# A fused attention and mixture-of-experts block in fp32: the expert output product in scaled fp16 halves, and w1 tiles between the last gates

## Chip, cores and metric

One Trainium2 chip (trn2), one of its cores. The metric is device microseconds of one launch, from inputs in HBM to the output in HBM. Smaller is better.

## What is computed

The reference takes `x` of 16 images, 96 channels, 16x16 pixels, all fp32, and does two residual layers, each behind a group norm of 32 groups:

```
x = x + attention(gn(x))      # 1x1 conv to q,k,v; depthwise 3x3; l2-normed channel attention, 8 heads; 1x1 conv
x = x + experts(gn(x))

scores  = softmax(x_flat @ gate_w + gate_b)            # 4 experts, per pixel
top_w   = softmax(top 2 of scores)
present = which experts occur anywhere at rank 0, at rank 1
coef    = present(rank, expert) * top_w(rank, pixel), summed over the ranks
hdn     = relu(w1[e] @ x + b1[e])                      # 4 x 96 hidden rows
out     = sum over e of coef[e] * (w2[e] @ hdn[e] + b2[e])
```

## The kernel before

The work goes by pairs of images: 8 pairs of 512 pixels (`T`). The engines are programmed by hand: each block (`tensor`, `vector`, `scalar`, `gpsimd`, `sync`) is one in-order list, and semaphores carry the dependences. Nothing is scheduled by a planner; the order of the code is the order of the queue.

First comes the attention layer, one pair per turn of a loop. PE makes q and k with the depthwise filter folded into nine shifted products (`conv_taps`, L721 to L737, fp16 halves of operands), projects v (`project_v`, L778), and makes the small products of the heads. DVE does the other eight taps of v (`taps`, L1150), the statistics (L1106) and the head arithmetic; `project_v(i + 1)` waits for all taps of pair i (`tap_done`). ACT makes the centre tap, copies q and k out of PSUM and rounds the normalised x to fp16; POOL subtracts for the low halves (L619, L624) and takes roots; SP packs the halves by DMA. The weights of the second layer are prepared in pairs 0 and 1: PE turns w1 and w2 (`prepare_late`, L699 to L702), ACT copies them (`copy_late`), DVE makes the low half of w1 (`low_w1`, L1086).

Then come the gates and the hidden layer. `gate(p)` (L835) is 4 fp32 products of four columns each. `first(h)`, h = 3 x pair + m for three blocks m of 128 hidden rows, is a w1 tile: three fp16 products of 512 columns (L850 to L852) into one of four banks, emptied by a relu of ACT (L511) or, for h in `RELU_DVE`, of DVE (L1215). DVE ranks the experts per pixel in two chunks of four pairs each (`gate_logits`, `gate_compare`, `gate_rank`, `gate_present`, `gate_scores`, `gate_weights`, `gate_parts`), where `present` of both chunks gives the counts on PE (L937, L940). `gate_parts` splits the two weights of a pixel into bf16 parts and copies them to `u_tok`, which PE turns into `u_sb` (`turn_u`, L928, and `take_u` on ACT, L524).

Last comes the second phase, per pair i (`second`, L975 and L979; DVE `mix` L1411 and `add` L1417): PE spreads the coefficients of the next pair over 128 rows (`coef`, L960), DVE multiplies them into the hidden values (`h_mixed`, two buffers), PE makes three fp32 products with w2 and one bf16 product for the bias, and DVE adds the result to x. POOL prepares the bias rows before it (L678 to L686). The last pair goes in two halves of 256 pixels (`last_second`, L989 and L990, L1436).

## Time and profile before

| | |
|---|---|
| median of 3 runs | 181.02 us (179.81 to 182.39) |
| the profiled execution | 178.98 us |
| its span in the trace | 177.2 us |
| PE, DVE, ACT, POOL busy | 161.3, 139.4, 89.1, 50.4 us |
| granted TensorE clock, mean | 0.981 |

All rows further down come from that one profiled execution. Times are us from the start of its span. A matmul's duration includes the way through the array, so neighbours overlap; the distance between their starts says what one costs PE in a stream. The granted clock is 1.00 at 2.4 GHz and 0.50 at 1.2 GHz. "[1.03 <-DVE present]" behind a row is idle time of the engine just before it, and what ended it.

### The profile page before, as it was taken

The page shows a single profiled execution, that of the slowest core. Times are in us where ns is not written, and L with a number is a line of the kernel's source. Part 1 is how long each engine was busy: PE and PEld are TensorE (multiplying, and loading weights), DVE is VectorE, ACT ScalarE, POOL GpSimd, SP SyncE. Part 2 cuts the span into 40 slices and gives each one's busy share as a digit, 9 for nine tenths or more (in the row PEclk, how much of TensorE's full clock was granted, in tenths as well). Part 3 has the DMA queues.
Part 4 walks back from the last instruction along what each step waited for, and adds up shares of the span by engine and source line. Part 5 has one row for each costly group of instructions (what it writes and reads, how often), then busy time and mean ns, then how long its engine had stood idle before and what let it go on. Part 6 is the DMA issues. An engine that isn't in the chain of part 4 may idle for free.

```text
span 177.2 us, 3598 instructions
## 1 busy us (share of the span) xinstructions
PE 161.3 (91%) x1313; PEld 119.1 (67%) x1313; DVE 139.4 (79%) x383; ACT 89.1 (50%) x206; POOL 50.4 (28%) x74
## 2 busy tenths in 40 slices
PE   0567988999989999899999999999979999999994
PEld 0556978999989899899999987667225423222232
DVE  2589999979999999988998894776894697566641
ACT  2083298749284592984954485636965323100000
POOL 5120222605143144432472363243520510000000
PEclk9999999999999999999999999999579999999999
DMA  6994123411405014040050000000000002011113
GB/s 149 240 226 97 29 72 80 113 42 36 117 0 137 17 35 121 0 135 19 10 145 0 6 0 0 2 4 0 0 0 0 4 0 62 27 44 44 48 45 89
DMA packets 8810, 9.71 MB, mean 55 GB/s; under 512 B 3640, under 2 KB 7512, under 8 KB 8792
## 3 DMA queue, kind: packets, MB, share of 16 engines
q1 hardware_dynamic: 8648, 9.25, 21.0%
q8 instruction: 10, 0.16, 0.4%
q10 hardware_dynamic: 144, 0.23, 0.3%
q14 instruction: 8, 0.07, 0.1%
HBM read 2.93 MB, written 1.57 MB: 25 GB/s over the span
## 4 chain that ended last, share of the span: by engine, by line
PE 51%; DVE 31%; issue 5%; ACT 4%; DMA 4%; POOL 2%; SPq 2%; DVEq 0%; POOLq 0%
DVE v_acc L1150 10%; PE mix_ps L975 7%; PE v_ps L975 5%; PE qk_ps L732 5%; PE qk_ps L734 5%; DVE stats L1106 3%; PE out_ps L821 3%; PE qk_ps L960 3%; DMA x_sb<-in_x 2%; PE sc_ps L786 2%; DVE wc L1037 2%; PE sc_ps L796 2%; POOL rstd L639 2%; PE qk_ps L737 2%; DMA x_c<-x_lo 1%
## 5 line engine op out<-in xcount | busy, mean ns | idle before, releaser
L1150 DVE SCALAR_TENSOR_TENSOR v_acc<-v_ps,v_taps,v_acc 96x576 f32<-96x576 f32 x64 | 51.8, 809 | 2.0 <-ACT v_acc L439 0.8
L732 PE MATMUL qk_ps<-w_a,x_a 128*128 128x192 f16 x243 | 46.6, 245 | 0.5 <-DMA x_c<-x_lo 0.5
L734 PE MATMUL qk_ps<-w_b,x_b 128*128 128x192 f16 x243 | 46.5, 245 | 0.0
L732 PEld LDWEIGHTS qk_ps<-w_a,x_a 128*128 128x128 f16 x243 | 24.6, 101 | 1.1 <-issue 0.8
L734 PEld LDWEIGHTS qk_ps<-w_b,x_b 128*128 128x128 f16 x243 | 23.6, 97 | 0.3
L737 PE MATMUL qk_ps<-w_c,x_c 96*128 96x192 f16 x81 | 20.1, 248 | 0.0
L630 POOL TENSOR_TENSOR sq_sum<-qk_sq 128x384 f32<-128x384 f32 x8 | 8.0, 999 | 30.5 <-ACT qk_sq L447 26.8
L1411 DVE TENSOR_TENSOR h_mixed<-hidden,qk_ps 128x512 f32<-128x512 f32 x16 | 10.7, 682 | 6.5 <-PE qk_ps L960 6.5
L485 ACT ACTIVATE sc_exp<-sc_qk,neg_max 96x12 f32<-96x12 f32 x16 | 4.7, 296 | 18.6 <-DVE neg_max L1189 18.5
L1106 DVE BATCH_NORM_STATS2 stats<-x_sb 96x6 f32<-96x256 f32 x32 | 11.6, 412 | 2.9 <-DMA x_sb<-in_x 2.7
L639 POOL TENSOR_TENSOR rstd<-var_eps,minus_half 96x4 f32<-96x4 f32 (+2 forms) x9 | 9.0, 996 | 17.1 <-DVE var_eps L1132 17.1
L975 PE MATMUL mix_ps<-h_mixed,w2T 128*96 128x512 f32 x24 | 13.2, 631 | 0.0
L634 POOL TENSOR_TENSOR rnorm<-norm,minus_half 96x4 f32<-96x4 f32 x8 | 8.1, 1013 | 15.3 <-DVE norm L1159 15.3
L624 POOL TENSOR_TENSOR xn_lo<-xn,xn_hi 96x512 f16<-96x512 f32 x8 | 9.3, 1166 | 10.3 <-ACT xn_hi L506 10.2
L619 POOL TENSOR_TENSOR x_lo<-xs,x_a 96x512 f16<-96x512 f32 x8 | 9.3, 1160 | 8.3 <-ACT x_a L467 8.3
L721 PE MATMUL qk_ps<-w_a,x_a 96*128 96x192 f16 x45 | 11.1, 246 | 0.5 <-ACT w_a L432 0.5
L459 ACT ACTIVATE xs<-x_sb,shift,rstd 96x256 f32<-96x256 f32 x16 | 8.7, 596 | 4.9 <-DVE shift L1138 4.9
L723 PE MATMUL qk_ps<-w_a,x_lo 96*128 96x192 f16 x45 | 11.1, 246 | 0.0
L722 PE MATMUL qk_ps<-w_b,x_a 96*128 96x192 f16 x45 | 11.1, 246 | 0.0
L975 PE MATMUL v_ps<-h_mixed,w2T 128*96 128x512 f32 x18 | 9.9, 631 | 0.0
L500 ACT ACTIVATE xn<-x_sb,shift,rstd 96x256 f32<-96x256 f32 x16 | 8.5, 590 | 1.1 <-DVE shift L1138 1.1
L446 ACT COPY qk_sb<-qk_ps 128x384 f32<-128x384 f32 x16 | 7.5, 469 | 3.1 <-PE sc_ps L796 2.9
(226 smaller groups left out, 365.6 us busy)
## 6 DMA issues: line engine op xcount, KB each, us to landing
x_b<-x_a SPq DMA_DIRECT2D x7, 324.0 KB, 3.1
x_sb<-in_x SPq DMA_DIRECT2D x8, 192.0 KB, 4.9
out<-xs SPq DMA_DIRECT2D x7, 192.0 KB, 2.1
x_a<-x_lo SPq DMA_DIRECT2D x7, 108.0 KB, 2.6
x_b<-x_lo SPq DMA_DIRECT2D x7, 108.0 KB, 2.3
x_c<-x_lo SPq DMA_DIRECT2D x21, 36.0 KB, 1.9
wdw_all<-in_L_conv_w_dw SPq DMA_DIRECT2D x1, 648.0 KB, 5.8
w_sb<-in_L_conv_w SPq DMA_DIRECT2D x2, 144.0 KB
```

What stands on the lines that cost most here:

```text
L619: eng.tensor_tensor(inner(x_lo[p], 1), xs[p][:, :].rearrange("c (b h w) -> c b h w", b=2, w=W), inner(x_a[p], 1), ALU.subtract).then_inc(l ...
L639: eng.tensor_tensor(rstd[:, lo:hi], var_eps[:, lo:hi], minus_half[:, 0:hi - lo], ALU.pow)\
L721: eng.matmul(to, hi, w_a[0:C, t, :], start=(t == 0), stop=False, skip_group_check=True)
L722: eng.matmul(to, hi, w_b[0:C, t, :], start=False, stop=False, skip_group_check=True)
L723: mm = eng.matmul(to, lo, w_a[0:C, t, :], start=False, stop=(t == TAPS - 1), skip_group_check=True)
L732: eng.matmul(to, window(x_a[p][:, dx, b], half, dy), w_a[:, t, :], start=(t == 0), stop=False, skip_group_check=True)
L734: mm = eng.matmul(to, window(x_b[p][:, dx, b], half, dy), w_b[:, t, :], start=False, stop=False, skip_group_check=True)
L737: mm = eng.matmul(to, window(x_c[p][:, b], half, dy), w_c[:, dy, :], start=False, stop=(t == TAPS - 1), skip_group_check=True)
L975: eng.matmul(to, w2T[:, m, :], h_mixed[i % 2][:, m, :], start=(m == 0), stop=False, skip_group_check=True)
L1106: s = eng.bn_stats(stats[:, at + b, :], x_sb[:, i, b * HW:(b + 1) * HW])
L1150: eng.scalar_tensor_tensor(out=v_acc[i % 3][:, :, :], in0=v_window(dy, dx), scalar=v_taps[:, t:t + 1], in1=v_acc[i % 3][:, :, :], op0=ALU. ...
L1411: eng.tensor_tensor(h_mixed[i % 2][:, m, :], hidden[:, i, m, :], coef_ps[m], ALU.mult)\
```

## The change

Part one, the gates: `first(10)` and `first(11)` go between gates 5, 6 and 7, and two more w1 tiles go ahead of the wait for `present`. ACT takes two relus earlier. On DVE `gate_parts` is divided into `gate_split` and the copies; for chunk 0 the copies go behind `gate_present(1)`.

Part two, the second phase: w2, with the factor of w1 already in it, is scaled per output channel to a largest value of 1024 and turned back; its first block stays fp32 (`w2_full`), the other two become fp16 halves (`w2_hi`, `w2_lo`). This takes a turn on PE, six operations on DVE, another turn, three copies on ACT and a subtraction on DVE, all in pairs 1 and 2. Per pair, ACT then rounds blocks 1 and 2 of `h_mixed` to fp16 (`high_mixed`), POOL subtracts for the low half, and PE makes one fp32 product, and hi x hi, lo x hi and hi x lo for each of two blocks. The product of the two low halves is not made. The addition multiplies by `w2_back`. The new buffers lie in `wc`, `wdw_all`, `x_a` and `x_b`, free by then. Before, no engine but PE and DVE worked on a pair in the second phase.

The diff, cut (declarations, semaphores and the second of two like places are left out):

```diff
+W2_SCALE = 1024.0
...
-                eng.copy(wprojT[:, :], out_ps[0:C, 0:C])
+                eng.copy(wprojT[:, :], out_ps[0:C, 0:C]).then_inc(late_set, 1)
                 for m in range(MT):
                     a = eng.activation(w2T[:, m, :], out_ps[:, C * (m + 1):C * (m + 2)], ACT.Copy,
                                        scale=w1_back[:, m:m + 1])
-                a.then_inc(late_set, 1)
+                a.then_inc(w2T_set, 1)
+
+            def high_w2():
+                eng.wait_ge(b2_turned, 1)
+                eng.copy(b2_rows[:, :], out_ps[0:EXPERTS, MT * C:(MT + 1) * C]).then_inc(b2_rows_set, 1)
+                eng.copy(w2_full[:, :], out_ps[:, 0:C])
+                eng.copy(w2_hi[:, 1:MT, :], out_ps[:, C:MT * C].rearrange("p (m o) -> p m o", m=MT - 1)).then_inc(w2_hi_set, 1)
+
+            def high_mixed(i):
+                wait(eng, y_done, i - 1)
+                wait(eng, h_lo_set, 2 * (i - 1))
+                for m in range(1, MT):
+                    eng.wait_ge(mixed_done, MT * i + m + 1)
+                    eng.copy(h_hi[i % 2][:, m, :], h_mixed[i % 2][:, m, :]).then_inc(h_hi_set, 1)
...
             for i in range(PAIRS):
                 centre_tap(i)
+                if i == 2:
+                    high_w2()
...
             normalise2(5)
             normalise2(6)
+            relu(7)
             normalise2(7)
-            relu(7)
+            relu(8)
...
                 relu(h)
             eng.wait_ge(bias_done, 1)
             eng.copy(bias32[:, :], small_ps[0:U, BIAS:BIAS + C]).then_inc(bias_copied, 1)
+            take_u(1)
+            high_mixed(0)
             top_exps(1)
-            take_u(1)
+            high_mixed(1)
             take_u(2)
             take_u(3)
+            for i in range(2, PAIRS):
+                high_mixed(i)
 
...
+            for i in range(PAIRS):
+                wait(eng, y_done, i - 1)
+                for m in range(1, MT):
+                    eng.wait_ge(h_hi_set, 2 * i + m)
+                    eng.tensor_tensor(h_lo[i % 2][:, m, :], h_mixed[i % 2][:, m, :], h_hi[i % 2][:, m, :],
+                                      ALU.subtract).then_inc(h_lo_set, 1)
...
+            def turn_w2():
+
+                eng.wait_ge(w2T_set, 1)
+                eng.wait_ge(w1_lo_set, 1)
+                for m in range(MT):
+                    eng.transpose(mix_ps[0:C, m * 128:(m + 1) * 128], w2T[:, m, :], const("ident", 128))
+                eng.transpose(mix_ps[0:C, ED:ED + EXPERTS], b2_sb[:, :], const("ident", EXPERTS)[:, 0:EXPERTS])\
+                   .then_inc(w2_turned, 1)
+
+            def turn_w2_again():
+                eng.wait_ge(b2_cols_set, 1)
+                for m in range(MT):
+                    eng.transpose(out_ps[:, m * C:(m + 1) * C], w2_scaled[:, m, :], const("ident", C)[:, 0:C])
+                eng.transpose(out_ps[0:EXPERTS, MT * C:(MT + 1) * C], b2_cols[:, :], const("ident", C)[:, 0:C])\
+                   .then_inc(b2_turned, 1)
...
-                    eng.wait_ge(w1_lo_set, 1)
+                    eng.wait_ge(b2_cols_set, 1)
...
+                if i == 1:
+                    turn_w2()
...
+                if i == 1:
+                    turn_w2_again()
...
             first(9)
             gate(5, 0, 8)
+            first(10)
             gate(6, 0, 8)
+            first(11)
             gate(7, 0, 8)
-            for h in (10, 11, 12, 13, 14, 15):
+            for h in range(12, 18):
                 first(h)
 
...
 
-            first(16)
-            first(17)
+            first(18)
+            first(19)
             eng.wait_ge(present_ready, 1)
             eng.wait_ge(norm_done, 9)
...
-            first(18)
-            first(19)
+            first(20)
+            first(21)
...
             turn_u(0)
             turn_u(1)
-            for h in range(20, HT):
+            for h in range(22, HT):
...
-                for m in range(MT):
+
+                coef(i + 1, 0)
+                eng.wait_ge(mixed_done, MT * i + 1)
+                eng.matmul(to, w2_full[:, :], h_mixed[i % 2][:, 0, :], start=True, stop=False, skip_group_check=True)
+                for m in range(1, MT):
                     coef(i + 1, m)
-                    eng.wait_ge(mixed_done, MT * i + m + 1)
-                    eng.matmul(to, w2T[:, m, :], h_mixed[i % 2][:, m, :], start=(m == 0), stop=False,
+                    eng.wait_ge(h_hi_set, 2 * i + m)
+                    eng.matmul(to, w2_hi[:, m, :], h_hi[i % 2][:, m, :], start=False, stop=False,
+                               skip_group_check=True)
+                    eng.matmul(to, w2_lo[:, m, :], h_hi[i % 2][:, m, :], start=False, stop=False,
                                skip_group_check=True)
                 if i == 0:
                     eng.wait_ge(bias_ready, 1)
-                eng.matmul(to, bias_u[:, :], u_sb[:, i * T:(i + 1) * T], start=False, stop=True,
-                           skip_group_check=True).then_inc(y_done, 1)
+                eng.matmul(to, bias_u[:, :], u_sb[:, i * T:(i + 1) * T], start=False, stop=False,
+                           skip_group_check=True)
+                for m in range(1, MT):
+                    eng.wait_ge(h_lo_set, 2 * i + m)
+                    mm = eng.matmul(to, w2_hi[:, m, :], h_lo[i % 2][:, m, :], start=False, stop=(m == MT - 1),
+                                    skip_group_check=True)
+                mm.then_inc(y_done, 1)
...
+            def scale_w2():
+
+                eng.wait_ge(w2_turned, 1)
+                eng.tensor_reduce(w2_top[:, :], mix_ps[0:C, 0:ED], AX.X, ALU.max, apply_absolute_value=True)\
+                   .then_inc(w2_step, 1)
+                eng.wait_ge(w2_step, 1)
+                eng.tensor_scalar(w2_floor[:, :], w2_top[:, :], TINY, 1.0 / W2_SCALE, ALU.max, ALU.mult)\
+                   .then_inc(w2_step, 1)
+                eng.wait_ge(w2_step, 2)
+                eng.reciprocal(w2_scale[:, :], w2_floor[:, :]).then_inc(w2_step, 1)
+                eng.wait_ge(w2_step, 3)
+                eng.reciprocal(w2_back[:, :], w2_scale[:, :])
+                eng.tensor_scalar(w2_scaled[:, :, :], mix_ps[0:C, 0:ED].rearrange("p (m d) -> p m d", m=MT),
+                                  w2_scale[:, 0:1], None, ALU.mult)
+                eng.tensor_scalar(b2_cols[:, :], mix_ps[0:C, ED:ED + EXPERTS], w2_scale[:, 0:1], None, ALU.mult)\
+                   .then_inc(b2_cols_set, 1)
+
+            def low_w2():
+                eng.wait_ge(w2_hi_set, 1)
+                eng.tensor_tensor(w2_lo[:, 1:MT, :], out_ps[:, C:MT * C].rearrange("p (m o) -> p m o", m=MT - 1),
+                                  w2_hi[:, 1:MT, :], ALU.subtract).then_inc(w2_lo_set, 1)
...
-            def gate_parts(c):
+            def gate_split(c):
                 t = chunk(c)
-                n = t.stop - t.start
                 step(eng.tensor_copy(tw_hi[:, :, t], top_w[:, :, t]))
                 step(eng.tensor_tensor(tw_rest[:, :, t], top_w[:, :, t], tw_hi[:, :, t], ALU.subtract))
                 step(eng.tensor_copy(tw_mid[:, :, t], tw_rest[:, :, t]))
                 step(eng.tensor_tensor(tw_lo[:, :, t], tw_rest[:, :, t], tw_mid[:, :, t], ALU.subtract))
+
+            def gate_parts(c):
...
+                if i == 2:
+                    low_w2()
...
-                taps(i, 6, 8)
+                taps(i, 6, 7)
+                if i == 1:
+                    scale_w2()
+                taps(i, 7, 8)
...
+            gate_split(0)
             gate_compare(1)
             gate_beaten(eng, 1)
             gate_rank(1)
             gate_present(1)
+            gate_parts(0)
             relu(16)
 
...
             def mix(i):
                 wait(eng, y_done, i - 1)
+                wait(eng, h_lo_set, 2 * (i - 1))
                 for m in range(MT):
...
             def add(i):
                 eng.wait_ge(y_done, i + 1)
                 wait(eng, stored[i % 2], 16 * (i // 2))
-                eng.tensor_tensor(out_sb[i % 2][:, :], x_sb[:, i, :], y_ps[i % 2][0:C, :], ALU.add)\
-                   .then_inc(y_taken, 1)
+                eng.scalar_tensor_tensor(out=out_sb[i % 2][:, :], in0=y_ps[i % 2][0:C, :], scalar=w2_back[:, 0:1],
+                                         in1=x_sb[:, i, :], op0=ALU.mult, op1=ALU.add).then_inc(y_taken, 1)
...
             gate_parts(1)
```

The order on each engine, as the two programs have it, at three places.

DVE at the end of pair 1, before, from the head factors on (`v_acc` is a tap, `x2` two in a row):

```order
L1172 TENSOR_TENSOR k_diag<-cst,rnorm 96x24
L1175 TENSOR_SCALAR q_fac<-rnorm,temp_sb 96x2
L1150 SCALAR_TENSOR_TENSOR v_acc<-v_ps,v_taps,v_acc 96x576 x2
L1138 SCALAR_TENSOR_TENSOR shift<-small_ps,rstd 96x4
L1180 TENSOR_TENSOR sc_k<-picked,sc_ps 96x24
L1186 TENSOR_TENSOR sc_qk<-sc_k,q_fac 96x24
```

and after (here `w_top` to `w_back` are the `w2_` tiles, whose numbers the listing leaves out):

```order
L1292 TENSOR_SCALAR q_fac<-rnorm,temp_sb 96x2
L1267 SCALAR_TENSOR_TENSOR v_acc<-v_ps,v_taps,v_acc 96x576
L1187 TENSOR_REDUCE w_top<-mix_ps 96x1
L1190 TENSOR_SCALAR w_floor<-w_top 96x1
L1193 RECIPROCAL w_scale<-w_floor 96x1
L1195 RECIPROCAL w_back<-w_scale 96x1
L1196 TENSOR_SCALAR w_scaled<-mix_ps,w_scale 96x384
L1198 TENSOR_SCALAR b_cols<-mix_ps,w_scale 96x4
L1267 SCALAR_TENSOR_TENSOR v_acc<-v_ps,v_taps,v_acc 96x576
L1255 SCALAR_TENSOR_TENSOR shift<-small_ps,rstd 96x4
L1297 TENSOR_TENSOR sc_k<-picked,sc_ps 96x24
```

Six operations now stand between tap 7 and tap 8.

PE around the last gates, before (`gate_w_sb` is a gate, three rows with `w_hi`, `w_lo`, `w_hi` a w1 tile):

```order
L852 MATMUL qk_ps<-xn_lo,w_hi 128x512
L835 MATMUL mix_ps<-gate_w_sb,xn_1 128x4 x4
L835 MATMUL mix_ps<-gate_w_sb,xn_2 128x4 x4
L835 MATMUL mix_ps<-gate_w_sb,xn_3 128x4 x4
L850 MATMUL v_ps<-xn_hi,w_hi 128x512
L851 MATMUL v_ps<-xn_hi,w_lo 128x512
L852 MATMUL v_ps<-xn_lo,w_hi 128x512
```

and after:

```order
L924 MATMUL qk_ps<-xn_lo,w_hi 128x512
L907 MATMUL mix_ps<-gate_w_sb,xn_1 128x4 x4
L922 MATMUL v_ps<-xn_hi,w_hi 128x512
L923 MATMUL v_ps<-xn_hi,w_lo 128x512
L924 MATMUL v_ps<-xn_lo,w_hi 128x512
L907 MATMUL mix_ps<-gate_w_sb,xn_2 128x4 x4
L922 MATMUL v_ps<-xn_hi,w_hi 128x512
L923 MATMUL v_ps<-xn_hi,w_lo 128x512
L924 MATMUL v_ps<-xn_lo,w_hi 128x512
L907 MATMUL mix_ps<-gate_w_sb,xn_3 128x4 x4
L922 MATMUL qk_ps<-xn_hi,w_hi 128x512
```

The three gates are apart by a w1 tile each.

ACT from the last relus on, before:

```order
L511 ACTIVATE hidden<-v_ps,b_scaled 128x512 x2
L597 COPY bias<-small_ps 12x96
L520 ACTIVATE top_exp<-top_diff 128x16
L524 COPY u_sb<-out_ps 12x1024
L524 COPY u_sb<-sc_ps 12x1024
L524 COPY u_sb<-out_ps 12x1024
```

and after (`x_a<-wc` and `x_a<-wdw_all` are `high_mixed` of an even and an odd pair):

```order
L552 ACTIVATE hidden<-v_ps,b_scaled 128x512 x2
L640 COPY bias<-small_ps 12x96
L565 COPY u_sb<-out_ps 12x1024
L469 CAST x_a<-wc 128x512 x2
L561 ACTIVATE top_exp<-top_diff 128x16
L469 CAST x_a<-wdw_all 128x512 x2
L565 COPY u_sb<-sc_ps 12x1024
L565 COPY u_sb<-out_ps 12x1024
L469 CAST x_a<-wc 128x512 x2
```

The roundings of pair 0 stand behind one `u_sb` copy, those of pair 1 ahead of the last two, and those of pair 2 behind all of them.

## Rows read from the trace of the kernel before

**Rows 1.** Chain of waits of core 0, 38 to 60 us, its shares by line.
```profile
by line: DVE v_acc L1150 46.2%; issue 14.4%; DVE stats L1106 11.6%; DVE picked L1167 4.3%; DVE attn L1197 4.0%; DVE x_sb L1155 2.8%; DVE masked L1163 2.5%; DVE mv L1120 2.1%; DVE sc_qk L1186 1.7%; DVE neg_max L1189 1.6%; ACT sc_exp L485 1.5
```

**Rows 2.** Timeline of DVE, pair 1: start, duration (us), line, operation, shapes.
```profile
21.98 0.17 DVE L1072 TENSOR_SCALAR w_row_max<-w_top 128x3 f32<-128x3 f32 x1
...
30.36 0.54 DVE L1086 TENSOR_TENSOR w_lo<-mix_ps,w_hi 96x384 f16<-96x384 f32 x1
...
33.62 0.34 DVE L1163 TENSOR_TENSOR masked<-sc_ps,cst 96x192 f32<-96x192 f32 x1
...
35.42 1.65 DVE L1150 SCALAR_TENSOR_TENSOR v_acc<-v_ps,v_taps,v_acc 96x576 f32<-96x576 f32 x2
```

**Rows 3.** Timeline of PE: weight transposes, and the projection of pair 2.
```profile
25.02 0.25 PE L699 MATMUL out_ps<-cst,wproj_sb 96*96 96x96 f32 x1
...
25.61 0.25 PE L702 MATMUL out_ps<-cst,w_sb 96*128 96x96 f32 x1
...
37.22 0.28 PE L778 MATMUL v_ps<-x_a,wv_hi 96*96 96x256 f16 x1
```

**Rows 4.** Timeline of ACT: one rounding of 96x512.
```profile
124.78 0.60 ACT L506 CAST xn_hi<-xn 96x512 f16<-96x512 f32 x1
```

**Rows 5.** Gate stretch: PE, then PEclk by window (start:end, busy times), DVE, POOL.
```profile
120.06 3.02 PE L835 MATMUL mix_ps<-gate_w_sb,xn 96*128 96x4 f32 x24 [0.31 <-ACT xn L500]
...
128.32 0.63 PE L852 MATMUL v_ps<-xn_lo,w_hi 96*128 96x512 f16 x1
...
131.14 0.38 PE L851 MATMUL qk_ps<-xn_hi,w_lo 96*128 96x512 f16 x1
131.35 0.38 PE L852 MATMUL qk_ps<-xn_lo,w_hi 96*128 96x512 f16 x1
132.76 0.20 PE L937 MATMUL small_ps<-present,ones 128*12 128x8 f32 x2 [1.03 <-DVE present L1256]
...
124.00:126.00 2.00, 2.00 (x6) 0.33 (x4) 1.49 (x7) 1.91 (x5) 0.54 (x1) 0.50 0.00 0
...
113.44 0.23 DVE L1230 TENSOR_TENSOR g_in<-logits,g_max 128x64 f32<-128x64 f32 x1
...
125.60 1.10 DVE L1230 TENSOR_TENSOR g_in<-logits,g_max 128x64 f32<-128x64 f32 x1
...
125.46 1.15 POOL L624 TENSOR_TENSOR xn_lo<-xn,xn_hi 96x512 f16<-96x512 f32 x1 [4.26 <-ACT xn_hi L506]
```

**Rows 6.** Timeline of DVE and POOL: taps beside a subtraction.
```profile
39.72 4.19 DVE L1150 SCALAR_TENSOR_TENSOR v_acc<-v_ps,v_taps,v_acc 96x576 f32<-96x576 f32 x5
...
41.45 1.16 POOL L619 TENSOR_TENSOR x_lo<-xs,x_a 96x512 f16<-96x512 f32 x1 [0.64 <-ACT x_a L467]
```

**Rows 7.** Second phase: busy times of one window, then PE, ACT, POOL, DVE.
```profile
160.00:170.00 10.00, 10.00 (x24) 2.50 (x24) 6.16 (x10) 0.00 (x0) 0.00 (x0) 1.00 0.21 59
...
144.00 0.41 PE L979 MATMUL mix_ps<-u_sb,bias_u 12*96 12x512 bf16 x1
...
149.61 0.39 PE L960 MATMUL qk_ps<-u_sb,spread 12*128 12x512 bf16 x1
149.92 1.10 PE L975 MATMUL mix_ps<-h_mixed,w2T 128*96 128x512 f32 x2
150.95 0.39 PE L960 MATMUL qk_ps<-u_sb,spread 12*128 12x512 bf16 x1
...
153.65 0.41 PE L979 MATMUL mix_ps<-u_sb,bias_u 12*96 12x512 bf16 x1
153.90 0.37 PE L960 MATMUL qk_ps<-u_sb,spread 12*128 12x512 bf16 x1
...
149.26 1.00 ACT L524 COPY u_sb<-sc_ps 12x1024 bf16<-12x1024 bf16 x1 [5.84 <-PE sc_ps L928]
...
142.13 0.40 POOL L686 TENSOR_TENSOR bias_u<-bias_d,bias_c 12x96 bf16<-12x96 f32 x1
...
174.61 0.42 DVE L1436 TENSOR_TENSOR xs<-x_sb,mix_ps 96x256 f32<-96x256 f32 x1 [1.28 <-PE mix_ps L990]
```

More of the change, by code:

```diff
@@ L112, in build @@
         w2T = sb("w2T", [128, MT, C])
+        w2_top = sb("w2_top", [C, 1])
+        w2_floor = sb("w2_floor", [C, 1])
+        w2_scale = sb("w2_scale", [C, 1])
+        w2_back = sb("w2_back", [C, 1])
+        w2_scaled = sb("w2_scaled", [C, MT, 128])
+        w2_full = sb("w2_full", [128, C])
+        w2_hi = sb("w2_hi", [128, MT, C], F16)
+        w2_lo = sb("w2_lo", [128, MT, C], F16)
+        b2_cols = sb("b2_cols", [C, EXPERTS])
+        b2_rows = sb("b2_rows", [EXPERTS, C])
         x_sb = sb("x_sb", [C, PAIRS, T])
@@ L579, in _ @@
             normalise2(6)
+            relu(7)
             normalise2(7)
-            relu(7)
+            relu(8)
             top_exps(0)
-            relu(8)
             high_xn2(5)
@@ L1285, in gate_parts @@
                 step(eng.tensor_tensor(tw_lo[:, :, t], tw_rest[:, :, t], tw_mid[:, :, t], ALU.subtract))
+            def gate_parts(c):
+                t = chunk(c)
+                n = t.stop - t.start
                 for part, at, k in ((tw_hi, 0, 3), (tw_mid, 3, 2), (tw_lo, 5, 1)):
```

57 lines of the change are left out of this document (40 added, 17 removed).

## The prediction

> **What bounds the kernel now.** I read the chain of waits first, then the timeline of each engine in three places, then the busy time by stage. The kernel has three stretches with different limits.
>
> From 25 to 60 us the chain runs on VectorE (DVE): between 38 and 60 us its largest parts are the depthwise taps `v_acc`, the statistics, and the small head operations, all DVE [rows 1]. TensorE (PE) is nearly as full, but it waits at the end of each pair: the projection of pair 2 starts at 37.22, 0.15 us after the last two taps of pair 1 end (35.42 + 1.65 = 37.07) [rows 2, 3]. So what is put into DVE's queue here goes to the end of the kernel, and what is put into PE's queue here is free only as far as DVE is later.
>
> Up to 133 us the limit is then the gate chain, again on DVE. PE runs the three last gates from 120.06 as 24 products of four columns, and a few us later its granted clock is 0.50, the 1.2 GHz level: a 512-column product takes 0.63 us at 128.32 and 0.38 at 131.14 [rows 5]. This looks like the price of the stretch, but PE then sits idle for 1.03 us until `present` is there, and starts the counts at 132.76 [rows 5]. PE at half clock was still early. What DVE lost is in the same group: `g_in` took 0.23 us at 113.44 and 1.10 at 125.60, and the long one ended (126.70) just after a POOL subtraction that had started at 125.46 ended (126.61). The Trainium skill has a rule for this ("SBUF — State Buffer", Who interferes with whom): a VectorE operation with two SBUF inputs and a GpSimd operation that reads SBUF shut each other out for a whole instruction. The trace agrees.
>
> From 140 us on PE is the limit: busy 10.00 us of 10 between 160 and 170, DVE 6.16 [rows 7]. A pair takes 4.29 us there, from the coefficient product at 149.61 to the same one of the next pair at 153.90. It is three times an fp32 product of 1.03 us (149.92 to 150.95) and a coefficient product of 0.32, plus 0.25 for the bias product [rows 7].
>
> **The preparation of the halves (pairs 1 and 2), on DVE.** `scale_w2` stands between tap 7 and tap 8 of pair 1, six operations. Reduction and scaling over 96x384 read from PSUM: the row of that width is `w_lo`, 0.54 us. The reduction must end before the next starts: 0.57; the scaling overlaps its neighbour by 0.08: 0.46. Three small ones in a chain at 0.17 and a gap of 0.03, the last without the gap: 0.5; `b2_cols` 0.1. Together 1.6 us. `low_w2` in pair 2 covers 128x192 like `masked` (0.34, of which 0.28 is not overlapped): 0.3. Sum 1.9 us, all in front of the tap on which the next projection waits [rows 2]. PE gets eight transposes; seven like them stand between 25.02 and 25.61 at 0.1 us each, so 0.8 us [rows 3]. They lie beside the 1.6 of DVE and cost nothing more while DVE is later; uncovered they cost 0.8. ScalarE (ACT) gets three copies (`high_w2`), about 0.5 us together since a 96x512 copy takes 0.60 [rows 4]; they stand behind DVE's chain in front of `take_qk` and the packing of pair 3, and might add 0.2. Bounds: 1.6 (if pair 2 absorbs its part) to 2.7 (if PE's transposes come on top). I take **+1.9**, the value of the DVE rows.
>
> **The gate stretch.** Gates 5, 6 and 7 get a w1 tile between them. Gate 7 ends 1.3 us later, near 124.3 (24 products from 120.06 took 3.0), still ahead of DVE, which works on those logits from 125.60. The clock may stay up, worth some 3 us of PE, but PE is not what is waited for. DVE's chain to `present` loses only the three copies to `u_tok`, an estimated 0.3 us of work of their own, three at 0.1 beside each other; the three POOL subtractions still meet two-input operations in it (`tw_rest`, `beats`, `tied` instead of the copies), so I let the three waits stand. Two more w1 tiles run before the wait, four instead of six remain behind it (saves 1.3). But the first of these four waits for `relu(16)`, now queued behind the `u_tok` copies (0.3) and itself some 0.7 long over its 512 columns, of which PE waits about 0.7, and ACT must still do five relus after `take_u(0)`, which comes 0.3 to 0.6 later against `present`. I take **-0.4** for the start of the second phase. Bounds: -3.2 (all POOL waits missed and the clock up) and +0.6 (ACT's queue decides and no wait is missed).
>
> **Second phase, first three pairs.** PE's products of a pair are now one fp32 (1.03), the coefficient product before it (0.32), and nine products at 16 bits: 131.14 to 131.35 is 0.21 each, so 1.94. Sum 3.29 instead of 4.29 [rows 5, 7]. But pair 0 ends with two low products that wait for POOL. POOL's bias work ends at 142.13 + 0.40 = 142.53 and only then come the two subtractions. One of 96x512 took 1.16 us [rows 6], width and types are the same here: 2.3 us, then the product, 0.4. That is 145.3, where before the bias product ended pair 0 at 144.41 [rows 7]: +0.9. Pair 1 has 1.0 less work on PE and takes it back. Pair 2 loses again, by ACT's order: `high_mixed(2)` stands behind `take_u(2)` and `take_u(3)`. Before, these began at 149.26 and took 1.9, to 151.2 [rows 7]. Add a rounding (0.60), two subtractions (2.3), the product (0.4) and four handovers (0.05 each): 154.7, where before pair 2 ended at 153.65 + 0.41 = 154.06. With the 0.4 of later starts that this chain inherits from pairs 0 and 1 and does not pass on (0.2), the second phase reaches the end of pair 2 **+1.1** later against its own start. Bounds 0.5 to 2.0.
>
> **Pairs 3 to 6.** Now the buffers decide. DVE was busy 6.16 of 10 us, so 2.6 a pair of 4.29 (three mixes and an addition, 0.65 each; that the addition now also multiplies changes little); ACT gets 2 x 0.6, POOL 2.3. The loop over two buffers (addition, three mixes, rounding, two subtractions, product) is 2.6 + 0.6 + 2.3 + 0.4 = 5.9, or 3.0 a pair. All are below 3.29, so PE stays the limit: 4 x 1.0 = **-4.0**. Bounds: -4.2, and 0 if the loop comes to 4.29 a pair.
>
> **Last pair.** Its products are 0.6 shorter, but no pair follows to hide the subtractions. They end some 2.1 us after pair 6; then follow the low product (0.3), the second half (1.4) and the addition (0.4): 4.3. Before, pair 6 ended at 154.06 + 4 x 4.29 = 171.2, and the last addition at 174.61 + 0.42 = 175.03 [rows 7]: 3.8 to 3.9. **+0.4**, bounds -0.6 and +1.0.
>
> **Sum.** 1.9 - 0.4 + 1.1 - 4.0 + 0.4 = -1.0 us. The profiled execution took 178.98 us (a span of 177.2 and 1.8 around it): 178.0. The median of the runs shown is 181.02, 2.0 above the profiled one, so the forecast for a median is 180.0.
>
> The same rule of the Trainium skill (that section) speaks against one part of the change: POOL, idle after 142.5 before, now reads SBUF through the second phase. By it the gate operations of the second chunk on DVE (`top_w`, `tw_rest` and others with two SBUF inputs) get waits of up to 1.2 us each, but the mixes, with one input in PSUM, get none. The rows say the same of the mixes: five taps (one input in PSUM) ran back to back in 4.19 us beside a POOL subtraction that kept its 1.16 [rows 6]. The gate operations have 1 to 2 us of slack before the turning of `u` needs them.
>
> **Rivals.** *Subtractions and mixes do shut each other out* (slower). Place: DVE and POOL in the pair loop. Then a pair costs 2.6 + 2.3 = 4.9 us, and pairs 3 to 6 give 4 x 0.6 = +2.4 instead of -4.0: 1.9 - 0.4 + 1.1 + 2.4 + 0.4 = +5.4, so 186.4. It decides as soon as a subtraction with its wait passes about 1.7 us; break-even is near 1.3, since six of them stand open on the path. Against it: rows 6. For it: no row has a mix beside POOL.
> *The gate stretch gives its waits back* (faster). Without the three POOL waits of some 0.9 each and the copies `present` comes up to 3 earlier, of which the start of the phase gets 2.8, and with the clock at 2.4 GHz PE is ready for it. Then -1.0 - 2.8 = -3.8: 177.2. For it: everything in this stretch moves by half a us and such meetings are a matter of position. Against it: three subtractions and mostly two-input operations on DVE leave few gaps.
> *The preparation is hidden* (the taps of pairs 1 and 2 have slack that the chain doesn't show): -1.0 - 1.9 = -2.9, 178.1. Against it: 0.15 us of slack at 37.22.
>
> **How the numbers follow.** Forecast 0.55 (its own range 178.8 to 181.5), gate stretch 0.17, preparation hidden 0.1, mutual exclusion 0.1; the rest is small losses on top (transposes uncovered, copies on ACT) up to 183. A measurement of this kernel tells about 2%, 3.6 us, from no change. Faster by that needs the gate rival, or it together with another: 0.16. Slower needs the exclusion: 0.11. The rest is 0.73. The range of 177.0 to 182.8 leaves out the better half of the gate rival and the exclusion. The three chances are 0.16, 0.73 and 0.11.
>
> **What would show it.** Right: project_v of pair 2 at 38.7 to 38.9; pair 4 and later shifted by 1.9; `present` near 134.2 (132.7 + 1.9 - 0.4); pair 3 to 6 at 3.3 us each with PE full; PE waiting for POOL at the ends of pairs 0, 2 and 7. Wrong: subtractions over 1.3 us, a period above 3.4, no shift at pair 3, or `present` off by more than 1 us.

## The result, and the profile after

The changed kernel took 185.85 us (median of 4 runs, 184.40 to 186.42), the kernel before beside it 180.42 (4 runs, 179.13 to 182.39). The ratio is 1.031, with a 95% interval of 1.021 to 1.041: slower, outside my range of 177.0 to 182.8. The profiled execution took 185.61 us with a span of 183.7, where before it was 178.98 and 177.2. Ratios here and below compare the runs that are left when the disturbed ones of each kernel are taken out; since part of the change's cost lies in how often such runs come, medians and lowest times over all runs stand beside them.

I read the page's row of TensorE's granted clock first (40 slices of the span, 9 is full speed). Before, then after:

```profile
PEclk9999999999999999999999999999579999999999
```

```profile
PEclk9999999999999999999999999995798555899999
```

Before, the clock falls once, in the gate stretch. After, it falls there too, although w1 tiles now stand between the gates, and then a second time for three slices and more. The windows of the changed kernel around it (start:end, length, then PE, weight loads, DVE, ACT, POOL busy, granted clock, DMA share and GB/s):

```profile
136.00:140.00 4.00, 3.43 (x24) 1.36 (x21) 0.60 (x1) 3.75 (x6) 0.00 (x0) 1.00 0.00 0
140.00:144.00 4.00, 4.00 (x11) 1.45 (x12) 3.29 (x11) 2.39 (x6) 3.25 (x10) 0.60 0.01 4
144.00:148.00 4.00, 4.00 (x9) 0.78 (x8) 3.06 (x5) 1.24 (x2) 4.00 (x4) 0.50 0.00 0
148.00:152.00 4.00, 4.00 (x7) 0.80 (x6) 3.28 (x11) 0.00 (x0) 0.17 (x1) 0.50 0.18 49
152.00:156.00 4.00, 4.00 (x16) 1.54 (x16) 1.40 (x2) 0.00 (x0) 0.00 (x0) 0.50 0.00 0
156.00:160.00 4.00, 4.00 (x18) 1.71 (x17) 1.41 (x3) 2.95 (x5) 1.20 (x2) 0.77 0.18 49
```

From 140 us on PE is busy in all of them, and every product takes longer. The clock is at 0.50, the 1.2 GHz level, from 140.8 to nearly 158 us. In the timeline of PE (start, duration, line, operation, shapes, idle before and its releaser) this is the coefficient product at 0.60 and the fp32 one at 2.02 us, where [rows 7] have 0.39 and 1.10:

```profile
39.02 0.28 PE L848 MATMUL v_ps<-x_a,wv_hi 96*96 96x256 f16 x1 [0.27 <-DVE v_acc L1267]
...
121.32 1.05 PE L907 MATMUL mix_ps<-gate_w_sb,xn 96*128 96x4 f32 x8 [0.31 <-ACT xn L541]
...
133.75 0.20 PE L1015 MATMUL small_ps<-present,ones 128*12 128x8 f32 x2
...
137.89 0.39 PE L922 MATMUL v_ps<-xn_hi,w_hi 96*128 96x512 f16 x1 [0.47 <-ACT hidden L552]
...
140.78 0.60 PE L1038 MATMUL qk_ps<-u_sb,spread 12*128 12x512 bf16 x1
141.31 2.02 PE L1053 MATMUL mix_ps<-wc,w_full 128*96 128x512 f32 x2
...
161.48 0.39 PE L1038 MATMUL qk_ps<-u_sb,spread 12*128 12x512 bf16 x1
161.79 1.10 PE L1053 MATMUL v_ps<-wdw_all,w_full 128*96 128x512 f32 x2
162.83 0.39 PE L1038 MATMUL qk_ps<-u_sb,spread 12*128 12x512 bf16 x1
163.14 0.42 PE L1057 MATMUL v_ps<-x_a,w_hi 128*96 128x512 f16 x1
163.40 0.38 PE L1059 MATMUL v_ps<-x_a,w_lo 128*96 128x512 f16 x1
163.71 0.39 PE L1038 MATMUL v_ps<-u_sb,spread 12*128 12x512 bf16 x1
...
164.93 0.63 PE L1067 MATMUL v_ps<-x_b,w_hi 128*96 128x512 f16 x2
165.49 0.38 PE L1038 MATMUL qk_ps<-u_sb,spread 12*128 12x512 bf16 x1
...
179.23 0.31 PE L1085 MATMUL v_ps<-x_b,w_hi 128*96 128x256 f16 x1 [0.30 <-POOL x_b L739]
```

The rows at 161.48 and 165.49 are the same product of two neighbouring pairs, at full clock: a pair takes 4.01 us, where it took 4.29 before [rows 7] and I had forecast 3.29. The starts of the products within it tell why: two products of w2 that stand together are 0.26 us apart (163.14, 163.40), but the next coefficient product comes 0.31 later, and the product of w2 behind it 0.31 later again, where I had counted 0.21 for each.

VectorE (DVE) shows the preparation and the gate chain:

```profile
36.38 0.55 DVE L1187 TENSOR_REDUCE w_top<-mix_ps 96x1 f32<-96x384 f32 x1
...
37.42 0.59 DVE L1196 TENSOR_SCALAR w_scaled<-mix_ps,w_scale 96x384 f32<-96x384 f32 x1
37.94 0.21 DVE L1198 TENSOR_SCALAR b_cols<-mix_ps,w_scale 96x4 f32<-96x4 f32 x1
38.07 0.80 DVE L1267 SCALAR_TENSOR_TENSOR v_acc<-v_ps,v_taps,v_acc 96x576 f32<-96x576 f32 x1
...
126.75 0.21 DVE L1323 SCALAR_TENSOR_TENSOR logits<-mix_ps,gate_b_sb 128x48 f32<-128x48 f32 x1 [0.49 <-PE mix_ps L907]
...
127.83 1.18 DVE L1400 CAST tw_mid<-tw_rest 128x32 bf16<-128x32 f32 x1
...
129.27 1.26 DVE L1356 TENSOR_TENSOR beats<-g_exp 128x256 f32<-128x256 f32 x1
...
133.01 0.17 DVE L1373 TENSOR_TENSOR present<-present 128x8 f32<-128x8 f32 x1
...
146.14 0.96 DVE L1392 TENSOR_SCALAR top_den<-top_exp 128x16 f32<-128x16 f32 x1
```

And GpSimd (POOL) the subtractions that I had feared for:

```profile
127.81 2.43 POOL L671 TENSOR_TENSOR xn_lo<-xn,xn_hi 96x512 f16<-96x512 f32 x2 [0.51 <-ACT xn_hi L547]
...
143.69 2.25 POOL L739 TENSOR_TENSOR x_b<-wc,x_a 128x512 f16<-128x512 f32 x2
```

Two subtractions in 2.25 us, beside mixes of DVE that still took 0.69: the mutual exclusion that was my slower rival did not come.

### The profile page after: what moved, and what is told of

Read it like the earlier page. It is cut to its first block, busy times and chain, and to the rows that moved or that the text cites. A ratio compares the mean times of both kernels' runs of the same rounds, so it can differ in the third digit from the quotient of the medians.

```text
span 183.7 us, 3713 instructions
## 1 busy us (share of the span) xinstructions
PE 167.7 (91%) x1339; PEld 122.8 (67%) x1339; DVE 142.6 (78%) x390; ACT 99.1 (54%) x225; POOL 68.4 (37%) x90
## 4 chain that ended last, share of the span: by engine, by line
PE 61%; DVE 25%; ACT 4%; issue 3%; DMA 2%; POOL 2%; POOLq 1%; DVEq 0%; ACTq 0%
DVE v_acc L1267 8%; PE qk_ps L802 7%; PE qk_ps L804 7%; PE out_ps L893 4%; PE qk_ps L1038 3%; DVE stats L1223 3%; PE mix_ps L1053 3%; PE qk_ps L807 2%; PE sc_ps L856 2%; PE mix_ps L907 2%; PE sc_ps L866 2%; DMA x_sb<-in_x 2%; PE v_ps L1053 2%; PE v_ps L848 2%; DVE wc L1132 2%
## 5 line engine op out<-in xcount | busy, mean ns | idle before, releaser
L739 POOL TENSOR_TENSOR x_b<-wc,x_a 128x512 f16<-128x512 f32 x8 | 9.1, 1152 | 14.0 <-ACT x_a L469 14.0
L739 POOL TENSOR_TENSOR x_b<-wdw_all,x_a 128x512 f16<-128x512 f32 x8 | 9.1, 1153 | 3.5 <-ACT x_a L469 3.5
L469 ACT CAST x_a<-wdw_all 128x512 f16<-128x512 f32 x8 | 4.9, 618 | 9.4 <-DVE wdw_all L1538 8.6
L1538 DVE TENSOR_TENSOR wc<-hidden,qk_ps 128x512 f32<-128x512 f32 x8 | 5.4, 681 | 4.7 <-PE qk_ps L1038 4.7
```

The costliest lines, as they stand in the source:

```text
L739: eng.tensor_tensor(h_lo[i % 2][:, m, :], h_mixed[i % 2][:, m, :], h_hi[i % 2][:, m, :], ALU.subtract).then_inc(h_lo_set, 1)
```

## The experiments

Each ran beside the kernel before on one chip, in four groups on three chips, so times of different groups are compared only roughly. The theory I began with: the second fall is what costs, and it comes because the stretch of PE just ahead of the second phase has become thin. Rival: it comes from the second phase itself.

**Each part alone.** Part one alone (gates, relus, tiles and the split `gate_parts`, in the kernel before):

```
             gate(5, 0, 8)
+            first(10)
             gate(6, 0, 8)
+            first(11)
             gate(7, 0, 8)
...
```

> The gate part of the change alone; the second phase stays three fp32 products per pair. Theory (the reordered gate stretch leaves TensorE too little to do just before the second phase, so the clock falls to 1.2 GHz near 139 us): it falls here too, and fp32 products of 1.03 us become 1.95 us for as long as it lasts; for three or four pairs that is 8 to 12 us, so 186 to 192 us against 180.4. Rival (the fp16 second phase itself brings the fall): the clock is 1.00 from 131 us on and the time is 180 +- 1 us.

183.06 us (4 runs), ratio 1.016 (1.006 to 1.026). Its profile has the second fall too, here from 139 to 146 us: 7 us, and not the three or four pairs behind the 186 to 192 us that I had expected. The second part alone (everything of part one undone in the changed kernel):

> The second-phase part alone (scaled halves, preparation, rounding and subtraction), with gates, relus and w1 tiles in the order of before. Theory: no fall near 140 us; the preparation costs 1.3, pairs take 4.0 instead of 4.3 us, pairs 0 and 2 lose about 2 together: 180 to 182 us. Rival (the second phase brings the fall itself): the clock falls as in the changed kernel and the time is 185 to 187 us.

184.06 us (4 runs, 180.02 to 184.35, no ratio), above the 180 to 182 of the theory. A second fall here as well, from about 146 to 156 us; in 144 to 148 PE was busy 3.08 of 4 us and waited for POOL's low halves of pair 0. The one run at 180.02 has the mean clock of a run without it (0.980). So neither part owns the fall. The preparation alone, its results unused and the second phase left as it was:

> The kernel before plus only the preparation of the halves of w2 (transposes, scaling, copies), whose results nothing uses: the second phase keeps its three fp32 products. Theory: the preparation costs what the trace of the changed kernel shows of it at the first gate, 1.3 us (121.32 against 120.06): 180.8 us against 179.5 before, and the clock falls once, as before. Rival (my prediction's sum of its operations): +1.9, 181.4. Other rival: the shift brings a second fall of the clock by itself: 182.5 or more.

182.30 us (10 runs, before 180.58), ratio 1.008 (1.002 to 1.013): 1.4 us, with the 1.3 of the trace (first of the last gates at 121.32 against 120.06) inside its interval of 0.4 to 2.4 and my 1.9 too. Only one of ten runs had a mean clock of at least 0.978, at 180.1; of the kernel before beside it 17 of 29. That is not the single fall of the theory, and the profiled run (182.61 us, mean clock 0.953) shows that a low mean clock need not be a second fall: its clock is at 0.50 from 16 to 24 us, in the attention layer, falls again in the gate stretch, and is 1.00 in the whole second phase.

**Two w1 tiles moved, nothing else.** In the kernel before:

```
             first(16)
             first(17)
+            first(18)
+            first(19)
             eng.wait_ge(present_ready, 1)
...
-            for h in range(20, HT):
+            for h in range(22, HT):
```

> The kernel before with two w1 tiles moved from behind the counts to the front of the wait for present (four instead of six stay behind it); nothing else. Theory (this makes the stretch of narrow products between the counts and the coefficients thin, and the clock falls behind it): a second fall at 138 to 148 us, as in e1_gates_only, mean clock 0.944 to 0.962 and 181.5 to 183.5 us. Rival (the second fall of e1_gates_only comes from the tiles between the gates or the order of the relus): one fall, 0.981, 179.0 to 179.8 us, as before.

183.72 us against 180.69 (6 runs, 180.51 upwards), ratio 1.016 (1.007 to 1.025). Its profile shows the clock down early in the first phase as well, which nothing in the edit explains, so I repeated it:

> The kernel of e12_tiles_early again (the kernel before with two w1 tiles moved ahead of the wait for present). Theory: second fall near 140 to 148 us in most runs, mean clock 0.944 to 0.971, 181 to 184 us, where the kernel before beside it has 0.981 and 179 us in about half of its runs. Rival (chance): the same spread as the kernel before.

182.48 against 179.50 (6 runs), ratio 1.012 (1.006 to 1.019). The windows of this second one:

```profile
132.00:136.00 4.00, 2.57 (x13) 0.93 (x12) 3.17 (x12) 0.00 (x0) 0.00 (x0) 0.73 0.00 0
136.00:140.00 4.00, 3.52 (x26) 1.76 (x24) 0.00 (x0) 2.57 (x4) 0.00 (x0) 0.85 0.00 0
```

Two tiles moved ahead of the wait for `present` cost 3 us in the median. Part is idle time of PE behind it (2.57 of 4 us busy, before 3.24), part a fall of the clock, but at 134 to 137 and not at 140 us as expected. This profiled run is the lowest of its six (180.97 us), so it doesn't show what the slower ones lost. The direction of the theory holds, the place doesn't. Putting the two tiles back in the changed kernel was expected to help accordingly:

```
-            first(18)
-            first(19)
             eng.wait_ge(present_ready, 1)
...
-            first(20)
-            first(21)
+            first(18)
+            first(19)
             eng.wait_ge(u_ready, 1)
...
-            for h in range(22, HT):
+            for h in range(20, HT):
```

> The changed kernel with only the w1 tiles 18 and 19 put back behind the counts (six behind present instead of four); tiles 10 and 11 stay between the gates, and the relus and the copies stay moved. Theory in its narrow form (these two tiles carry the clock over the stretch 134 to 140): no second fall, 179 to 182 us. Rival (the copies and relus moved, or the phase itself): fall as before, 184 to 187 us.

184.60 us (4 runs), ratio 1.030 (1.020 to 1.040), with the clock at 0.60 in 148 to 152 us, and in this profile at 0.50 in 20 to 24 us too. It didn't help: a miss for the theory in its narrow form.

**Filling the stretch.** Six extra fp32 products of ones (128 rows by 128 columns, as the kernel has elsewhere) between the turning of `u` and the last two w1 tiles:

```
             turn_u(1)
+            eng.wait_ge(logit_free, PAIRS)
+            keep_warm(6, mix_ps[:, 256:512])
             for h in range(22, HT):
```

> The changed kernel with six more idle products of 128 columns on TensorE (1.7 us) between the turning of u and the last two w1 tiles. Theory: they fill the half microsecond that TensorE waits there and keep the clock up; they cost up to 1.2 us themselves and save 7: 179 to 181 us. Rival (the clock follows from the products of the second phase): 185.9 plus 1 = 186 to 187.5 us.

182.87 us (10 runs), ratio 1.003 (0.995 to 1.010). Three runs, the profiled one among them, came at 180.0 to 180.2 with a mean clock of 0.981; six at 182.8 to 183.2 with 0.962 to 0.968 (none of these has a trace). None of the 4 runs of the changed kernel had been under 184.4. Its windows, for the same times as those of the changed kernel above:

```profile
136.00:140.00 4.00, 4.00 (x29) 2.35 (x26) 0.17 (x1) 4.00 (x8) 0.00 (x0) 1.00 0.02 4
140.00:144.00 4.00, 4.00 (x16) 1.59 (x15) 3.83 (x11) 2.32 (x4) 3.50 (x10) 1.00 0.00 0
144.00:148.00 4.00, 3.08 (x9) 0.94 (x9) 4.00 (x3) 1.22 (x2) 3.97 (x4) 1.00 0.00 0
```

That is the second phase at full clock, and so the trace on which the rest of my sum can be read (next section). The same six products in the kernel before, as a control:

> The kernel before with the same six extra products of ones in the same place (behind the turning of u, ahead of the last w1 tiles). Theory (they only keep the second fall away, which the kernel before seldom has): no gain, 179.5 to 180.5 us. Rival (they gain in any kernel, so that e4_warm's gain says nothing of the change): under 178.5 us.

181.23 against 180.58 (10 runs), ratio 1.007 (1.001 to 1.013): they gain nothing there. Its profiled run (182.01 us, mean clock 0.962) has no second fall either; its clock is at 0.50 from 119 to 132 us, ahead of the extra products. Then the place. Four more products in the waits of pair 0 for POOL:

> e4_warm with four more extra products of ones (one and three) in the two waits for GpSimd at the end of pair 0, in all 0.93 us there, where 0.9 us of them fit. Theory (in 6 of 10 runs e4_warm had a second fall, mean clock 0.962, 2.9 us longer, which comes from this wait): nearly all runs show a mean clock of 0.981 and 180.0 to 180.4 us. Rival (the second fall doesn't hang on this wait): as often 182.9 us as in e4_warm.

182.44 (12 runs), ratio 1.006 (1.000 to 1.011), four runs of twelve at 179.9 to 180.6: as e4_warm, so the rival holds: what the other runs lose doesn't hang on this wait. That it is a second fall was my assumption, from the mean clock alone. And the six products behind 140 us instead of ahead of it:

```
-            keep_warm(3, mix_ps[:, 256:512])
+            keep_warm(9, mix_ps[:, 256:512])
             second(0)
```

> The changed kernel with e4_warm's six extra products of ones behind the first three coefficient products (at 140 us) and not between the turning of u and the last two w1 tiles (at 136.5 us). Theory (what counts is that the stretch ahead of 140 us is full): the fall stays, and the extra products come on top with 1.3 to 1.6 us: 185 to 187 us. Rival (extra full-height products anywhere there keep the clock up): as e4_warm, 180.0 to 183 us.

183.03 (12 runs), ratio 1.006 (0.999 to 1.013), lowest 179.99. Again the rival: their place within these few microseconds made no difference that the runs show. Its profiled execution (182.56 us, mean clock 0.962) has no second fall, but a first one twice as long:

```profile
120.00:124.00 4.00, 4.00 (x16) 2.57 (x14) 2.38 (x9) 3.98 (x8) 2.11 (x3) 0.50 0.00 0
124.00:128.00 4.00, 4.00 (x17) 2.99 (x16) 1.63 (x8) 2.61 (x6) 1.49 (x2) 0.50 0.00 0
128.00:132.00 4.00, 4.00 (x13) 2.12 (x14) 2.37 (x10) 1.86 (x5) 1.25 (x2) 0.50 0.00 0
```

Time and mean clock are those of the six slower runs of e4_warm, so these too may have lost their 3 us ahead of the second phase.

**The changed kernel once more**, to see how often it loses the time:

> The changed kernel itself, beside the two others. Theory (the second fall of the clock is this kernel's own, by its thin stretch at 134 to 140 us): nearly every run with a mean clock of 0.962 or less, median 184 to 186 us, none at 180. Rival (a matter of chance or of the chip on which it was first timed): a good part of the runs with a mean clock of 0.981 and near 180 us.

185.24 us in the median of 12 runs, against 179.50 of 23 runs of the kernel before, a difference of 5.7. But two runs came at 179.91 and 179.92, with a mean clock of 0.981, and the ratio, which rests on three of the twelve, is 1.004 (0.997 to 1.011). "None at 180" was wrong; the loss is frequent, not certain. A third run with 0.981 took 185.22, so the clock isn't all that varies. The profiled run is the slowest, 213.82 us, with a granted clock of 0.75 in 20 to 24, 60 to 64 and 112 to 116 us, which no other profile here has; I read nothing else from it.

**The changes of weights.** In e4_warm, pairs 1 to 6, with the three coefficient products and the bias product side by side between the fp32 product and the others:

```
+                eng.matmul(to, w2_full[:, :], h_mixed[i % 2][:, 0, :], ...)
+                for m in range(MT):
+                    coef(i + 1, m)
+                eng.matmul(to, bias_u[:, :], u_sb[:, i * T:(i + 1) * T], ...)
                 for m in range(1, MT):
-                    coef(i + 1, m)
                     eng.matmul(to, w2_hi[:, m, :], h_hi[i % 2][:, m, :], ...)
```

> e4_warm with the products of 12 rows of a pair side by side (three coefficient products, then the bias product, then the 16-bit products of w2), in pairs 1 to 6: two changes a pair between 12-row and 128-row weights instead of eight. Theory (a change costs some 0.1 us over the 0.21 of a product): the pair's period falls from 4.01 to 3.3 to 3.45 us, six pairs save 3.4 to 4.3 us less what other waits take back: near 177 us against 180.0 for e4_warm without disturbance. Rival (these products cost 0.25 to 0.3 wherever they stand): the period stays above 3.9 and the time at 180.

181.55 us (6 runs, before 180.58), lowest 177.73, ratio 0.988 (0.978 to 0.999) from two of the six. PE, one pair:

```profile
158.92 1.02 PE L1055 MATMUL mix_ps<-wc,w_full 128*96 128x512 f32 x2
159.87 0.60 PE L1040 MATMUL qk_ps<-u_sb,spread 12*128 12x512 bf16 x2
160.32 0.37 PE L1040 MATMUL v_ps<-u_sb,spread 12*128 12x512 bf16 x1
160.53 0.38 PE L1058 MATMUL mix_ps<-u_sb,bias_u 12*96 12x512 bf16 x1
160.84 0.42 PE L1062 MATMUL mix_ps<-x_a,w_hi 128*96 128x512 f16 x1
161.09 0.38 PE L1064 MATMUL mix_ps<-x_a,w_lo 128*96 128x512 f16 x1
...
162.17 1.02 PE L1055 MATMUL v_ps<-wdw_all,w_full 128*96 128x512 f32 x2
```

The period is 3.25 us with the very same products, instead of 4.01. Eight changes between weights of 12 and of 128 rows have become two, so one costs 0.76 / 6 = 0.13 us. The weight loads of the changed kernel show where it goes:

```profile
162.82 0.09 PEld L1038 LDWEIGHTS qk_ps<-u_sb,spread 12*128 12x128 bf16 x1 [0.79 <-issue]
163.14 0.12 PEld L1057 LDWEIGHTS v_ps<-x_a,w_hi 128*96 128x96 f16 x1 [0.23 <-issue]
163.18 0.12 PEld L1059 LDWEIGHTS v_ps<-x_a,w_lo 128*96 128x96 f16 x1
```

The load at a change starts with its own product (163.14 and 163.14; 162.82 and 162.83), while that of `w_lo` starts at 163.18, well ahead of its product at 163.40. The Trainium skill says that PE pulls a weight load ahead of products in flight when their row groups don't conflict or when it goes to the background weights ("TensorE: Matmul & The Clock Gate", The mechanism). The trace agrees for loads of equal height; between 12 and 128 rows it shows no pulling ahead, which is compatible with a conflict of row groups, but not a proof of it.

Unequal height isn't the whole condition. Three loads of the kernel before:

```profile
72.00 0.10 PEld L737 LDWEIGHTS qk_ps<-w_c,x_c 96*128 96x128 f16 x1
134.39 0.43 PEld L928 LDWEIGHTS sc_ps<-ident_bf,u_tok 128*12 128x12 bf16 x8 [0.42 <-issue]
138.08 0.10 PEld L952 LDWEIGHTS small_ps<-b_sb,on_cols 4*12 4x12 f32 x2 [0.42 <-issue]
```

Weights of 96 rows between weights of 128, all fp16, are loaded ahead (72.00, product at 72.08), and the products stay 0.08 to 0.09 us apart. The turning of `u`, 128 rows by 12 columns in bf16 behind 96 rows in fp16, starts with its load, 0.31 us after the product before it (134.09, 134.40); so does the small product of 4 rows by 12 columns in fp32 (137.77, 138.08). In the pair, each change between 12 and 128 rows is also one between bf16 and fp16 or fp32. So the 0.13 us is shown for these changes; whether rows, columns or type make it was not separated.

The same grouping without the extra products:

> The changed kernel with the 12-row products grouped as in e6_grouped, without the extra products of ones. Theory (two separate losses, the changes of weights and the second fall of the clock): six periods shorter by 0.76 us at full clock, so 4 to 5 us under the changed kernel's 185.9: 181 to 182 us, with the second fall still there (mean clock 0.93 to 0.96). Rival (the shorter pair loop leaves PE waiting and brings further falls): above 183 us.

183.72 (6 runs, 180.87 upwards), ratio 1.014 (1.004 to 1.023). That is 1.5 to 2.1 us under the two medians of the changed kernel, not the 4 to 5 expected. A second fall is there in its profile (0.50 in 148 to 152), and the time is the rival's; whether more falls came with the shorter period, one trace doesn't tell.

**The best version.** In addition ScalarE's (ACT's) rounding of pair 2 ahead of the last two copies of turned `u`:

```
+            high_mixed(2)
             take_u(2)
             take_u(3)
-            for i in range(2, PAIRS):
+            for i in range(3, PAIRS):
```

> e6_grouped with ScalarE's rounding of pair 2 ahead of the copies of the last two turned quarters of u. Theory: in e6_grouped pair 2's low products waited 0.70 us for GpSimd, whose subtractions come behind the rounding, and that behind 1.9 us of copies; with the rounding first this wait goes: 0.5 to 0.9 us less, 177.0 us undisturbed against 177.7. Rival (the copies are then late for the coefficients of pair 4, or GpSimd's two subtractions were the limit anyway): 177.7 or more.

180.11 us (12 runs) against 180.69, lowest 177.23, ratio 0.992 (0.986 to 0.997). PE's wait in pair 2 fell from 0.70 to 0.40 us. This version is faster than the kernel before by some 0.8% by this ratio, by 0.3% in the median, and it is 5 us under the medians of the changed kernel. The same with part one of the change undone:

> e10_round_first with part one of the change undone: the gates 5 to 7 side by side, VectorE's and ScalarE's order of before around them, the w1 tiles of before. Theory (tiles between the gates do nothing for the end of the gate chain, and one fall of the clock stays in either): within 0.5 us of e10_round_first. Rival (part one is worth the 0.8 us by which the counts came earlier against the shift in the changed kernel): 0.8 us longer than e10_round_first.

180.54 (12 runs), lowest 178.50, ratio 1.003 (0.998 to 1.007). In the two profiles the second phase begins 1.36 us later without part one (the coefficient product of pair 0 at 140.89 against 139.53), and the lowest runs differ by 1.27, the medians by 0.43. So part one is worth about 1.3 us in a run without further loss, by the two tiles that PE no longer has behind the counts; with the six extra products PE is what this stretch waits for.

## Why the prediction was wrong, step by step

Forecast: the profiled execution would come 1.0 us lower, at 178.0. It came 6.6 higher. The trace of e4_warm, whose second phase ran at full clock, splits this in two. From the start of pair 3 to the last addition's end it took 20.03 us (156.05 to 176.08), as did the changed kernel (161.48 to 181.51); from the start of pair 0 to that of pair 3 it took 15.10 us (140.95 to 156.05), the changed kernel 20.70 (140.78 to 161.48). **The second fall cost 5.6 us.** Without it the profiled execution would have come to 185.6 - 5.6 = 180.0, and the two lowest runs of the repeat did, at 179.9.

- **The clock: the step that failed.** I wrote "The clock may stay up, worth some 3 us of PE, but PE is not what is waited for", and priced every product of the second phase at full clock. I took the clock as a thing of the gate stretch, from one profile, and gave no rival and no room in the range to a fall in the stretch where PE is the limit and each microsecond at 1.2 GHz costs up to half a microsecond (17 us cost 5.6 here, since the slower products fill the waits of 0.2 to 0.7 us for POOL and ACT that e4_warm has in the same pairs). Even in the gate stretch the sentence holds only for a short fall: e13_warm_later, with the clock down from 120 on, took 2.6 us more than its lowest run. And the first fall didn't stay away: it came at 123.7 with tiles between the gates, made gate 7 late (it ended at 126.6, forecast 124.3), and DVE waited 0.49 us for it (row at 126.75).
- **Pairs 3 to 6: right in direction, mis-sized.** 4.01 us a pair instead of 3.29; the term of -4.0 measures 4 x (4.01 - 4.28) = -1.1. The rows for it were in the profile: the coefficient product cost 0.31 before an fp32 product in [rows 7], the tiles' products 0.21 in [rows 5], and I used the second for products that now alternate with 12-row ones. e6_grouped shows the 3.25 that my sum described.
- **Pairs 0 to 2: right in the sum, by luck in its parts.** +1.1 forecast; 15.10 in e4_warm against 13.94 before (139.96 to 153.90): +1.2. Pair 0 cost +0.91, as forecast. But pair 1 gave back 0.29 and not all of it (146.15 to 151.22 against 144.25 to 149.61, by the same changes of weights), and pair 2 cost +0.54 and not about 1 (151.22 to 156.05 against 149.61 to 153.90).
- **Preparation: its size right, its cover missed.** DVE's chain took 1.69 us (36.38 to 38.07; forecast 1.6), the projection of pair 2 started 1.80 later (39.02 against 37.22, forecast 38.7 to 38.9), that of pair 5 still 1.96 later (72.18 against 70.22), but that of pair 6 only 1.26 (83.33 against 82.07). Before, PE had waited for a transfer behind the projection of pair 5 (PE's timeline of the kernel before), and this wait is gone after:

```profile
71.59 0.24 PE L732 MATMUL qk_ps<-w_a,x_a 128*128 128x192 f16 x1 [0.55 <-DMA x_c<-x_lo]
```

- **Gate stretch: -0.4 forecast.** `present` moved by 0.47 us (133.01 against 132.54) where everything ahead had moved by 1.26: -0.8 to that point. I had let three waits for POOL stand. Before, they are `g_in` with 1.10 [rows 5] and these two:

```profile
127.27 1.06 DVE L1285 TENSOR_TENSOR tw_lo<-tw_rest,tw_mid 128x32 bf16<-128x32 f32 x1
128.49 1.23 DVE L1287 COPY u_tok<-tw_mid 128x64 bf16<-128x64 bf16 x1
```

After there are only two, `tw_mid` with 1.18 and `beats` with 1.26, beside POOL's subtractions from 127.81. From `logits` to `present` DVE took 6.26 us (126.75 to 133.01) against 7.44 (125.10 to 132.54): 0.3 less for the copies, 0.9 for the wait that didn't come, so one of the three waits of my faster rival. The late gate 7 took 0.4 of it back. The counts then stood behind the added w1 tiles until 133.75, 0.99 later than before [rows 5]. The pair loop starts 0.82 later in all (140.78 against 139.96), forecast 1.5 (1.9 - 0.4).
- **Last pair: +0.4 forecast.** From the start of pair 6 to the end of the last addition e4_warm took 8.00 us, before 8.29 (166.74 to 175.03). The pair itself accounts for -0.27 of this, which leaves about 0.
- **The sum at full clock:** 0.8 + 1.2 - 1.1 = +0.9, so 179.9. The single number of the forecast was near this for the wrong reasons: -4.0 was 2.9 too good, the terms ahead of the pair loop 0.7 and that of the last pair 0.4 too dear, and it had 2.0 added for the median.
- **The rivals.** Mutual exclusion: no (two subtractions in 2.25 us beside mixes of 0.69). The same rule of the Trainium skill ("SBUF — State Buffer", Who interferes with whom) had named the gate operations of the second chunk instead; `top_w`, with two SBUF inputs, took 0.79 us. The trace agrees there. It also shows waits that I had not counted, in operations with one input: `top_den` took 0.96 and the cast `tw_mid` 1.18 beside POOL, where the same cast took 0.18 in the second chunk (148.68). The gate stretch gave back one wait of three (above). The preparation was not hidden: 1.80 us at pair 2.

What brings the second fall is settled only in part. Shown: it needs none of the fp16 products (e1_gates_only has none), and the profiles of both parts alone have it (e1_gates_only, e2_split_only). Beyond these traces there are only mean clocks, and a mean clock doesn't say where the clock fell: e5_prep_only lost it in the attention layer, e7_warm_control and e13_warm_later ahead of the second phase. A mean clock of at least 0.978, as in the profile before, was had by

- 57 of 90 runs of the kernel before beside these experiments, and 6 of 10 with the six extra products (e7_warm_control);
- 3 of 16 runs of the changed kernel, 2 of 18 with only one part of the change or the preparation (e1, e2, e5), none of 10 in e3 and e9;
- 3 of 12 runs of the kernel before with two tiles moved (e12, e14), against 33 of 48 beside them;
- 23 of 64 runs with the six extra products and the second part.

That a low mean clock is more frequent with the change and with the moved tiles is clear of chance in these numbers. That the extra products make it rarer again isn't (23 of 64 against 3 of 16); for it speaks the median, 182.4 to 183.0 in e4, e8 and e13 against 185.2 and 185.9. Which of the small stretches decides, and why, the runs don't tell.

## What to carry to other kernels

Before you cost a change on PE, look where PE is the limit and ask what stands ahead of it: products moved out of a stretch that has waits can cost more than a change saves, here 2 to 3 us for two tiles, of which the traces show part as idle time and part as a lower clock. Take the mean clocks of several runs for the price and not one profile, and traces of the slow ones too for the place. And when products of few rows (here also of another type) stand among products of full height, group them: here the same work took 3.25 us a pair grouped and 4.01 alternating.
